# The triangle of the causal mask is added in PSUM by VectorE instead of by a matmul, and ScalarE's order of two stages is swapped

## What is computed

```python
xn = _layernorm(x)
S = einsum('bhqd,bhkd->bhqk', Q, K) / sqrt(32)      # 16 heads of 32, 1024 queries and keys
S = where(causal, S, -1e30)
attn = (softmax(S) @ V) merged over heads @ Wo.T
ffn = 2 of 8 routed experts (width 352) + a shared expert (width 704)
out = x + attn + ffn
```

## Time and profile before

| | |
|---|---|
| median of 3 runs | 1165.86 us (1165.05 to 1168.9) |
| the profiled execution | 1170.92 us, of which its span is 1169.1 us |
| mean granted TensorE clock | 0.963 of full speed |
| busy in the span | PE 1055.6, DVE 769.1, ACT 647.0, POOL 505.2 us |
| first and last score matmul (L1433) | at 220.0 and 772.9 us |

### The profile page before, as it was taken

How to read it: one execution, slowest core, us unless ns; L and a number is a source line. 1 busy time by engine, 2 the same in 40 slices (tenths; PEclk the granted TensorE clock), 3 DMA queues, 4 the chain that set the end, 5 groups by cost and what they waited for, 6 DMA issues and landing times. The chain is left out here.

```text
span 1169.1 us, 19196 instructions
## 1 busy us (share of the span) xinstructions
PE 1055.6 (90%) x5379; PEld 819.2 (70%) x5380; DVE 769.1 (66%) x1729; ACT 647.0 (55%) x1291; POOL 505.2 (43%) x566
## 2 busy tenths in 40 slices
PE   5979995978999999999999999989879999999994
PEld 4857873756677776777777777757668777777773
DVE  6832344646578878877777777555367777777782
ACT  4523220445677777777787777851155555555551
POOL 0001815389656555555655565540013333334331
PEclk9989996989899999999999999989989999999998
DMA  5987978578145265444343444038793334433332
GB/s 190 316 320 294 153 268 264 107 119 152 37 145 145 53 202 99 146 115 146 100 112 116 145 133 130 2 119 284 234 370 64 66 72 72 72 65 66 71 69 36
DMA packets 109559, 165.68 MB, mean 142 GB/s; under 512 B 54016, under 2 KB 64512, under 8 KB 106272
## 3 DMA queue, kind: packets, MB, share of 16 engines
q1 hardware_dynamic: 99136, 143.92, 43.0%
q0 software_dynamic: 9760, 20.49, 9.9%
q10 hardware_dynamic: 576, 0.26, 0.1%
HBM read 103.35 MB, written 61.28 MB: 141 GB/s over the span
## 5 line engine op out<-in xcount | busy, mean ns | idle before, releaser
L1175 POOL TENSOR_TENSOR prob_lo<-prob,prob_hi 128x512 fp32r<-128x512 f32 (+2 forms) x320 | 308.2, 977 | 224.2 <-ACT prob_hi L1220 169.4
L1213 ACT ACTIVATE prob<-ps_s 128x512 f32<-128x512 f32 (+3 forms) x384 | 188.2, 490 | 141.1 <-PE ps_s L1438 95.9
L1220 ACT ACTIVATE prob_hi<-prob 128x512 fp32r<-128x512 f32 (+3 forms) x384 | 198.5, 517 | 12.7 <-ACT row_stage L1194 12.7
L1283 DVE CUSTOM_DVE_ANT_0 ps_m<-ps_m,causal 128x384 f32<-128x384 f32 (+3 forms) x256 | 126.8, 496 | 75.2 <-PE ps_m L1409 74.1
L1851 DVE TENSOR_TENSOR rw_lo<-gu_sb,rw_hi 128x704 fp32r<-128x704 f32 x156 | 138.9, 893 | 48.9 <-ACT rw_hi L1786 44.3
L1765 POOL DMA_INDIRECT out<-work,rows x39 | 61.6, 1580 | 251.6 <-DVE rows L1812 131.5
L1409 PE MATMUL ps_m<-ks,qs 96*128 96x512 f32 (+3 forms) x384 | 140.0, 366 | 13.8 <-DMA ks<-qk_hi 12.8
L1786 ACT ACTIVATE rw_hi<-gu_sb 128x704 fp32r x156 | 123.4, 793 | 47.9 <-PE ps_ru L1884 32.4
L1433 PE MATMUL ps_s<-qs,ks 97*128 97x512 f32 (+3 forms) x384 | 138.3, 360 | 2.7 <-ACT prob L1213 2.6
L1456 PE MATMUL ps_o<-prob_hi,vs 128*66 128x512 f32 (+3 forms) x384 | 132.1, 344 | 9.3 <-issue 5.3
L1287 DVE TENSOR_REDUCE maxima<-ps_m 128x1 f32<-128x512 f32 x128 | 86.8, 686 | 69.2 <-PE ps_m L1409 68.8
(11 more groups left out here) (211 smaller groups left out, 2416.2 us busy)
## 6 DMA issues: line engine op xcount, KB each, us to landing
xt<-xt_blocks SPq DMA_DIRECT2D x8, 2048.0 KB, 8.5
v_rows<-work SPq DMA_DIRECT2D x16, 512.0 KB, 2.9
qk_hi<-work SPq DMA_DIRECT2D x8, 1024.0 KB, 4.1
qk_lo<-work SPq DMA_DIRECT2D x8, 1024.0 KB, 7.0
qs<-qk_hi SPq DMA_DIRECT2D x64, 128.0 KB, 2.9
ks<-qk_hi SPq DMA_DIRECT2D x64, 128.0 KB, 3.1
vs<-v_rows SPq DMA_DIRECT2D x32, 256.0 KB, 5.0
out<-y_acc SPq DMA_DIRECT2D x32, 256.0 KB, 3.5
```

What stands on the lines that cost most here:

```text
L1175: nc.gpsimd.tensor_tensor(prob_lo[:, s % NPL, 0:w], prob[:, s % NP, 0:w], prob_hi[:, s % NPH, 0:w].bitcast(F32), ALU.subtract).then_inc(lo ...
L1213: nc.scalar.activation(prob[:, s % NP, 0:w], ps_s[s % NS][:, 0:w], ACT.Exp, scale=SCALE).then_inc(exp_done, 1)
L1220: nc.scalar.activation(prob_hi[:, s % NPH, 0:w], prob[:, s % NP, 0:w], ACT.Copy).then_inc(hi_ready, 1)
L1283: nc.vector.tensor_tensor_reduce(ps_m[s % NM][:, 0:w], ps_m[s % NM][:, 0:w], causal[:, TBW - w:], 1.0, MASKED, ALU.add, ALU.max, maxima[:, ...
```

## The change

The second matmul of a diagonal score block goes, and with it `eye`. In its place DVE adds `late`, now plain float32, to the first 128 columns of `ps_s`, as its first work of the step, and ACT's exponential of such a block waits for the new semaphore `masked` instead of `s_done`. On ACT the high half of the step before is taken ahead of the exponential, not behind it. The planner no longer counts 60 ns for a diagonal block, so a few filler matmuls move between steps. POOL builds `late` directly, with two copies fewer at the start.

```diff
@@ step_cost
-            cost += span(n)[1] / 2.25 + (60 if n in DIAGONAL else 0)
+            cost += span(n)[1] / 2.25
@@ attend_phase
-        late = sbuf("late", [P, P], F32R)
-        eye = sbuf("eye", [P, P], F32R)
+        late = sbuf("late", [P, P])
+        masked = sem("masked")
@@ gpsimd: the constants
-                scratch = prob[:, 0, 0:P]
-                nc.gpsimd.memset(scratch, 0.0).then_inc(consts_zeroed, 1)
+                nc.gpsimd.memset(late[:, :], 0.0).then_inc(consts_zeroed, 1)
...
-                nc.gpsimd.tensor_copy(late[:, :], scratch).then_inc(consts_ready, 1)
-                nc.gpsimd.tensor_copy(eye[:, :], ident[:, :]).then_inc(consts_ready, 1)
@@ scalar
                 def exp(s):
                     first, w = span(s % NB)
-                    act.wait_ge(s_done, s + 1)
+                    if s % NB in DIAGONAL:
+                        act.wait_ge(masked, count(DIAGONAL, s))
+                    else:
+                        act.wait_ge(s_done, s + 1)
...
-                    for lag, stage in ((COPY, copy_o), (EXP, exp), (ROW + 1, row), (HI, hi),
+                    for lag, stage in ((COPY, copy_o), (HI, hi), (EXP, exp), (ROW + 1, row),
                                        (ROW + 6, load_row)):
@@ vector
+                def mask(s):
+                    if s % NB in DIAGONAL:
+                        dve.wait_ge(s_done, s + 1)
+                        nc.vector.tensor_tensor(ps_s[s % NS][:, 0:P], ps_s[s % NS][:, 0:P],
+                                                late[:, :], ALU.add).then_inc(masked, 1)
...
                 for s in range(ALL):
+                    if 0 <= s - AHEAD < STEPS:
+                        mask(s - AHEAD)
                     gate(s)
@@ tensor: score
-                    diagonal = s % NB in DIAGONAL
-                    last = nc.tensor.matmul(ps_s[s % NS][:, 0:w],
-                                            ks[0:ROWS + 1, c, kt * P:(kt + 1) * P],
-                                            qs[0:ROWS + 1, c, q0:q0 + w], start=True,
-                                            stop=not diagonal)
-                    if diagonal:
-                        last = nc.tensor.matmul(ps_s[s % NS][:, 0:P], eye[:, :], late[:, :],
-                                                start=False, stop=True)
-                    last.then_inc(s_done, 1)
+                    nc.tensor.matmul(ps_s[s % NS][:, 0:w],
+                                     ks[0:ROWS + 1, c, kt * P:(kt + 1) * P],
+                                     qs[0:ROWS + 1, c, q0:q0 + w], start=True, stop=True
+                                     ).then_inc(s_done, 1)
```

More of the change, by code:

```diff
@@ L1148, in place @@
                             yield
-                scratch = prob[:, 0, 0:P]
-                nc.gpsimd.memset(scratch, 0.0).then_inc(consts_zeroed, 1)
+                nc.gpsimd.memset(late[:, :], 0.0).then_inc(consts_zeroed, 1)
                 pool.wait_ge(consts_zeroed, 1)
-                nc.gpsimd.affine_select(out=scratch, in_=scratch, compare_op=ALU.is_ge,
+                nc.gpsimd.affine_select(out=late[:, :], in_=late[:, :], compare_op=ALU.is_ge,
                                         fill=MASKED, base=0, pattern=[[1, P]],
-                                        channel_multiplier=-1).then_inc(consts_zeroed, 1)
+                                        channel_multiplier=-1).then_inc(consts_ready, 1)
+                nc.gpsimd.memset(causal[:, :], 0.0).then_inc(consts_zeroed, 1)
                 pool.wait_ge(consts_zeroed, 2)
-                nc.gpsimd.tensor_copy(late[:, :], scratch).then_inc(consts_ready, 1)
-                nc.gpsimd.tensor_copy(eye[:, :], ident[:, :]).then_inc(consts_ready, 1)
-                nc.gpsimd.memset(causal[:, :], 0.0).then_inc(consts_zeroed, 1)
-                pool.wait_ge(consts_zeroed, 3)
                 nc.gpsimd.affine_select(out=causal[:, TBW - P:], in_=causal[:, TBW - P:],
@@ L1280, in maximum @@
                     if s == 0:
-                        dve.wait_ge(consts_ready, 5)
+                        dve.wait_ge(consts_ready, 4)
                     if k0 + w == P * (t + 1):
@@ L1528, in shared @@
                             down(unit, m - UP_END[-1])
-                pe.wait_ge(consts_ready, 5)
+                pe.wait_ge(consts_ready, 4)
                 for s in range(ALL):
```

## The result

The changed kernel takes 1208.6 us (median; 1204.6 to 1211.6) against 1165.5 before: a ratio of 1.0389, 95% interval 1.0351 to 1.0427. It is 43 us slower, where 1166 and a range of 1151 to 1181 were forecast.

The account below looks back on a forecast made before the run. PE was taken to bound most of a head, DVE's chain the part before the row; per head +0.40 - 0.43 - 0.05 + 0.15 = +0.07 us, with -2.2 for other masks -0.2 in all: 1166 us, range 1151 to 1181.

Parts of the forecast that it names:

- The wait of the exponential: Exponentials delayed by DVE's mask mostly fit before the score two steps on; stalls 0.15 us a head, bounds 0 and 0.60.
- Rival 2: Slower: late masks delay exponentials and PE stalls at the score two steps on; 1173 to 1184 us, chance 0.33.
- the ring: Mask, exponential and the score two steps on, with two buffers; DVE and ACT each get 1.6 us more a head.
- The planner: 0.24 filler matmuls a steady head move into steps 0 to 2, under PE's wait: 0.05 us a head gained.
- The matmuls taken out: Mask matmuls gone from PE's part, steps 3, 5, 7, 9, 11: 0.43 us a head gained, bounds 0.30 and 0.60.
- The mask's cost on DVE: A mask holds DVE 0.20 us; those of steps 0 and 1 lengthen the chain by 0.40 us a head.
- rival 3: Slower by a little: the mask holds DVE its full 0.28 us in the chain; 1170 us, chance 0.05.
- The chain from step 11's maximum to the end of L1336: DVE's work before PE turns the row of maxima; forecast to grow from 4.17 to 4.6 us.
- rival 1: Faster: ACT's swap moves POOL's starts, so DVE's merge L1291 no longer waits for POOL; 1145, likelier 1155 us, chance 0.25.
- the idle time before the row: PE's idle before the transpose of the row of maxima, forecast to grow from 0.70 to about 1.3 us a head.
- The margins of the exponential: Step 7's exponential ends near 572.33, score of step 9 starts 572.49; step 0's ends 562.55, score of step 2 starts 562.59.
- The order on ACT: High half directly behind its exponential must wait for its end: 1.6 us a head on ACT, costing nothing.

Follow-up runs that it names:

- e11: The changed kernel with the planner's 60 ns for a diagonal block back and nothing else: 1196.9 us, ratio 1.0296.
- e6: The changed kernel with ScalarE's copy of the output one step earlier, ahead of the exponential that waits for the mask: 1160.1 us, ratio 0.9948.
- e9: e6 with the planner's 60 ns for a diagonal block back: 1153.2 us, ratio 0.9915.
- e1: The kernel before with only ScalarE's order changed, high half ahead of the exponential: 1160.0 us, ratio 0.9983.
- e8: e3 with the planner's 60 ns for a diagonal block back: 1150.1 us, ratio 0.9881.
- e3: The changed kernel without the mask of the scores, exponential waiting for the score alone, its scale an eighth (output not the reference's): 1161.1 us, ratio 0.9984.
- e4: As e3, but VectorE does a reduction in the place of each mask and nobody waits for it: 1171.3 us, ratio 1.0077.
- e12: The kernel before with only the copy of the output one step earlier on ScalarE, ahead of the exponential: 1157.2 us, ratio 0.9907.
- e10: e1 (mask by the matmul, old planner, high half first) with the copy of the output one step earlier: 1152.8 us, ratio 0.9912.
- e5: The changed kernel with VectorE's low halves done behind the next mask instead of ahead of it: 1196.4 us, ratio 1.0263.
- e2: The changed kernel with ScalarE's old order (exponential, row, then high half of the step before): 1221.0 us, ratio 1.0527.

## Why the prediction was wrong

The change taken apart, each part as the difference of two ratios to the kernel before, in us as that share of 1165.5. The parts depend on the order in which they are taken: the planner's edit costs 0.9% in the changed kernel (e11) but 0.3% once the copy is early (e6 against e9). The sum is 45 us, where the two medians differ by 43.

```
ScalarE's order alone            e1                    -0.2%   -2 us
256 matmuls off TensorE          e8 against e1         -1.0%  -12 us
the planner's edit               e3 against e8         +1.0%  +12 us
the mask's load on VectorE       e4 against e3         +0.9%  +11 us
exponential waits for the mask   changed against e4    +3.1%  +36 us
sum                                                    +3.9%  +45 us
```

**The wait of the exponential: the step that failed.** The prediction listed what is "queued behind the late exponential on ACT": its own high half, then POOL, then values six steps on, "covered". It left out what ACT does next at the head of steps 6 and 10, the copy of the output, which PE needs at once: there is one `ps_o`, and the next output starts in that very step. So the delay of an exponential does not have six steps of cover; twice in a head, when it stands ahead of a copy, it has none. The term was 0.15 us a head with a bound of 0.60; the dependency costs 36 us, over 28 heads 1.3 us a head. e6 is the proof: the copy taken out of that queue, with the mask, the load and the wait all left in place, brings 1208.6 down to 1160.1. By the ratios that is 4.4%, of which 0.9% is what the same move gives the kernel before (e12); the 3.5% left are near the 3.1% of the table. And with the copy early, the changed kernel with the old counts (e9) equals the matmul mask (e10). The trace of before held the hint: its late starts have 0.21 us a head before those value matmuls. In e12 they are 0.04, which makes 5 of its 10 us.

**Rival 2** had the sign and the ring, "the exponential becomes the ring", and priced it at 1173 to 1184; its sign, more than 5 us of PE idle for the exponential, came true with 21.4. It looked only at the score two steps on, whose late start is 0.73 us a head in step 9. That one is real, but e5 and e6 show that it is no cause by itself: moving the low half ended it and left 1196; moving the copy took it down to 0.11.

**The planner** was costed at 0.05 us a head gained. The 0.24 filler matmuls a steady head come out of the formula as was said, but the rest of the program was not looked at: the counts also set when units of the shared expert end, and SP's loads and DVE's splits hang on that. It came out 11 us the other way.

**The matmuls taken out** were 0.43 us a head, 12 us, and 2 more for the other 32 masks: 14; measured 12. **The mask's cost on DVE** was 0.28 us long and 0.20 start to start; it is 0.30 on average and 0.20. From DVE's timeline of the changed kernel, steps 11 to 1:

```profile
571.30 0.42 DVE L1282 CUSTOM_DVE_ANT_0 ps_m<-ps_m,causal 128x256 f32<-128x256 f32 x1
...
571.80 0.54 DVE L1290 TENSOR_TENSOR maxima<-maxima 128x4 f32<-128x4 f32 x1
572.26 0.29 DVE L1297 TENSOR_TENSOR ps_s<-ps_s,late 128x128 f32<-128x128 f32 x1
572.47 0.67 DVE L1356 SCALAR_TENSOR_TENSOR hid<-gated,ps_f 96x512 f32<-96x512 f32 x1
...
573.93 0.28 DVE L1297 TENSOR_TENSOR ps_s<-ps_s,late 128x128 f32<-128x128 f32 x1
574.13 0.67 DVE L1286 TENSOR_REDUCE maxima<-ps_m 128x1 f32<-128x512 f32 x1
...
575.03 0.41 DVE L1336 TENSOR_TENSOR work<-o_sum,o_inv 128x128 f32<-128x128 f32 x1
```

The next instruction starts 0.21 and 0.20 us after the mask, and over all 256 masks the median is 0.20. So rival 3 is out, and with it the strict reading of the rule that the prediction took from the Trainium skill, "VectorE: DVE Perf Modes", section "The DRAIN you can't avoid". The chain from step 11's maximum to the end of L1336 is 4.14 us (571.30 to 575.44), where 4.6 was forecast and 4.17 stood before: two masks make it 0.41 longer, but the merge holds DVE 0.46 (571.80 to 572.26) instead of 0.78, and L1336 takes 0.41 instead of 0.48. Each chain has one stage of the shared expert in it. So **rival 1** was right in its mechanism as well: its sign, L1291 well under 0.75 us, came true with a median of 0.31, and the idle time before the row stayed at 0.70 us where about 1.3 was forecast.

**The margins of the exponential** were a little larger than written: 571.51 + 0.28 + 0.49 is 572.28, not 572.33, and 561.63 + 0.28 + 0.60 is 562.51, not 562.55. The forecast does not hang on that; in the head shown above the mask of step 7 started 1.73 us after the low half of step 4 had begun in front of it (392.33 to 394.06).

**The order on ACT** was costed at nothing, and e1 measures 0.998. With the mask on DVE it is worth 1.3% (e2 against the changed kernel).

**Open:** why the value matmuls of steps 6 and 10 wait twice as long in e2 as in the changed kernel was not pursued; and which of the late starts fed which. No run has the copy early and the low half of step 4 long, so how much of e6's gain comes by way of the shorter low half is not separated. It is not the main part: e2 has the short one and takes 1221 us, and e5, which puts the masks ahead of it, gains 12 us of the 48.

## What to carry to other kernels

When a stage gets a new wait, list everything that its engine does behind it up to the next step's first stages, and for each ask who needs it and how soon; the one with the shortest cover sets the price, not the one that follows in the data flow. A stage that frees a single buffer belongs ahead of the stage that may wait. And a planner's constant is not local: before changing it, see which loads and splits cross a border by it.

## What the runs showed of the hardware

A Vector instruction with both inputs in SBUF can take far longer beside GpSimd's work: the 128x512 low half 0.68 us or 1.81, the 128x512 weight split 0.69 or 1.78, the merge of 4 columns 0.16 in e1 and up to 1.10 in the earlier trace rows. The mask, with one input in PSUM, stays at 0.28 to 0.34 us in every run that has it; this agrees with what the prediction cited from the Trainium skill, "SBUF — State Buffer", section "Who interferes with whom". That the stall can be 1.1 us, most of one GpSimd instruction of that size (1.3 us), was not expected.

Which of the two pays goes with who starts first, and a few hundredths of a us are enough. Two low halves of DVE in the changed kernel, each with the one of POOL that starts beside it:

```profile
392.30 1.29 POOL L1171 TENSOR_TENSOR prob_lo<-prob,prob_hi 128x512 fp32r<-128x512 f32 x1
392.33 1.81 DVE L1307 TENSOR_TENSOR prob_lo<-prob,prob_hi 128x512 fp32r<-128x512 f32 x1
...
490.35 0.68 DVE L1307 TENSOR_TENSOR prob_lo<-prob,prob_hi 128x512 fp32r<-128x512 f32 x1
...
490.55 1.63 POOL L1171 TENSOR_TENSOR prob_lo<-prob,prob_hi 128x512 fp32r<-128x512 f32 x1 [0.19 <-issue]
```

In that trace there are 51 such pairs of 128x512, with starts within 0.6 us of each other. In all 22 where POOL started 0.02 to 0.04 us ahead, DVE took 1.80 to 1.82 us and POOL about 1.29. In all 29 where POOL started 0.02 to 0.50 us behind, DVE took 0.68 to 0.85 and POOL 1.49 to 1.81. So a change of order on a third engine, as ACT's in e1, can move a stall of 1.1 us onto a Vector instruction or off it.
